# Chunk 0 of the weights in two transfers, its stationary columns rounded on ScalarE, four rounded products first

## What is computed

```
y    = x @ W.T + b + 2 * (x @ A[slot]) @ B[slot]        # slot = itok[sequence], rank 16
base = y @ W_base.T + b_base;  logits = y @ W_router.T
w    = softmax over the two largest logits of 8, placed at their experts
out  = x + base + 2 * sum_e w_e * (y @ A_e.T) @ B_e.T
```

## Time and profile before

| | |
|---|---|
| median of 3 runs | 66.52 us |
| the profiled execution | 66.64 us |
| its span | 64.9 us |
| PE busy | 61.1 us (94%) |
| DVE busy | 36.9 us (57%) |
| ACT busy | 22.9 us (35%) |
| POOL busy | 17.1 us (26%) |

### The profile page before, as it was taken

One profiled execution on the slowest core, in us unless ns is written; L12 is line 12 of the kernel. 1 busy time (PEld: TensorE's weight loads), 2 busy tenths in 40 slices (PEclk: granted clock), 3 DMA queues, 4 the chain that ended last, 5 costly groups with the idle time before them and its releaser, 6 DMA issues.

```text
span 64.9 us, 1174 instructions
## 1 busy us (share of the span) xinstructions
PE 61.1 (94%) x422; PEld 60.2 (93%) x422; DVE 36.9 (57%) x105; ACT 22.9 (35%) x46; POOL 17.1 (26%) x29
## 2 busy tenths in 40 slices
PE   5989999999999999999999999999999999999920
PEld 5969999999999999989999999999999999999910
DVE  0057959999899685126805675012768255956040
ACT  0669078606999898054121100020201131020000
POOL 6700000000799997759360000011000000000000
PEclk9999999999999999999999999999999999999999
DMA  0899998303899305155659997500044000033513
GB/s 0 222 358 353 402 407 267 115 5 96 225 316 374 128 6 130 37 130 126 146 90 399 351 375 282 200 0 0 0 171 154 9 0 0 0 121 121 229 48 127
DMA packets 6025, 10.57 MB, mean 163 GB/s; under 512 B 755, under 2 KB 2547, under 8 KB 6020
## 3 DMA queue, kind: packets, MB, share of 16 engines
q1 hardware_dynamic: 5730, 10.17, 47.1%
q10 hardware_dynamic: 290, 0.33, 1.5%
HBM read 7.37 MB, written 2.10 MB: 146 GB/s over the span
## 4 chain that ended last, share of the span: by engine, by line
PE 89%; DMA 4%; ACT 1%; DVE 1%; DVEq 0%; issue 0%
PE ps L693 26%; PE ps L601 23%; PE ps L705 19%; PE ps L753 8%; PE ps L662 5%; DMA wt<-w_chunks 4%; PE ps L728 2%; PE ps L733 2%; PE ps L739 1%; PE ps L716 1%; ACT wt_hi L352 1%; DVE xn L554 1%; DVEq L71 0%; PE ps L672 0%
## 5 line engine op out<-in xcount | busy, mean ns | idle before, releaser
L693 PE MATMUL ps<-am,x_hi 128*128 128x384 f32 x64 | 16.6, 340 | 0.0
L705 PE MATMUL ps<-bm,x_hi 128*128 128x280 f32 x64 | 13.0, 297 | 0.0
L693 PEld LDWEIGHTS ps<-am,x_hi 128*128 128x128 f32 x64 | 11.4, 188 | 0.0
L693 PE MATMUL ps<-am,x_lo 128*128 128x384 f32 x32 | 10.8, 338 | 0.0
L319 POOL TENSOR_TENSOR x_lo<-xt,x_hi 128x512 fp32r<-128x512 f32 x8 | 10.8, 1361 | 0.0
L705 PEld LDWEIGHTS ps<-bm,x_hi 128*128 128x128 f32 x64 | 10.1, 189 | 0.0
L705 PE MATMUL ps<-bm,x_lo 128*128 128x280 f32 x32 | 9.3, 290 | 0.0
L554 DVE TENSOR_TENSOR xn<-ps,xn 128x280 f32<-128x280 f32 (+1 forms) x16 | 6.1, 418 | 2.7 <-PE ps L753 2.6
L601 PE MATMUL ps<-wt_hi 128*128 128x280 f32 (+1 forms) x32 | 7.0, 316 | 0.2 <-ACT wt_hi L352 0.2
L601 PE MATMUL ps<-wt_lo,wt_hi 128*128 128x280 f32 (+1 forms) x32 | 7.0, 314 | 0.0
L326 POOL CAST am<-as_hl 128x128 fp32r<-128x128 f32 x8 | 2.9, 373 | 14.1 <-PE ps L693 14.1
(11 more groups left out here) (74 smaller groups left out, 99.4 us busy)
## 6 DMA issues: line engine op xcount, KB each, us to landing
xt<-x_t SPq DMA_DIRECT2D x4, 512.0 KB, 6.5
xn<-x_n SPq DMA_DIRECT2D x4, 512.0 KB, 5.5
out_n<-xn SPq DMA_DIRECT2D x7, 256.0 KB, 2.1
wt<-w_chunks SPq DMA_DIRECT2D x2, 582.0 KB, 6.2
g_st<-g_hl SPq DMA_DIRECT2D x12, 81.0 KB, 2.1
ab<-adapters SPq DMA_DIRECT2D x8, 64.0 KB, 2.7
wt<-w_chunks SPq DMA_DIRECT2D x1, 326.0 KB, 4.2
wt<-w_chunks SPq DMA_DIRECT2D x2, 128.0 KB, 3.0
```

Of the source, the lines that this page charges most:

```text
L693: last = mm(a_bank(b)[:, 0:R + WA], v[:, p, i, tok], am[:, i, level, at:at + R + WA], start=(i == 0 and n == 0), stop=False, skip_group_ch ...
L705: mm(b_bank(b)[:, 0:QB], v[:, p, i, tok], bm[:, i, level, :], start=(i == 0 and n == 0), stop=False, skip_group_check=True)
```

## The change

Chunk 0 comes in two transfers, one from SP (all 512 stationary columns) and one from ScalarE (all 648 moving columns and the bias). ScalarE rounds the stationary columns in two halves, blocks 2 and 3 first. VectorE no longer rounds any of them; it takes the remainders of the stationary columns ahead of those of the 368 moving columns. TensorE runs hi by hi for all four blocks, waiting for each half, and then hi by lo for all four.

```diff
-W0_PIECES = [slice(D // 2, D), slice(0, D // 2), slice(D, D + QB), slice(D + QB, CB)]
+W0_PIECES = [slice(0, D), slice(D, CB)]
 # SyncE
-            for n in (0, 1):
-                sp.dma_start(wt[:, 0, W0_PIECES[n]], w[:, 0, W0_PIECES[n]]).then_inc(w0_in[n], 16)
+            sp.dma_start(wt[:, 0, W0_PIECES[0]], w[:, 0, W0_PIECES[0]]).then_inc(w0_in[0], 16)
 # ScalarE
-            for n in (2, 3):
-                act.dma_start(wt[:, 0, W0_PIECES[n]], w[:, 0, W0_PIECES[n]]).then_inc(w0_in[n], 16)
+            act.dma_start(wt[:, 0, W0_PIECES[1]], w[:, 0, W0_PIECES[1]]).then_inc(w0_in[1], 16)
             act.dma_start(idx_sb[:], idx).then_inc(idx_in, 16)
             act.wait_ge(w0_in[0], 16)
-            for i in (2, 3):
-                c = slice(i * P, (i + 1) * P)
+            for c in (slice(D // 2, D), slice(0, D // 2)):
                 hi(wt_hi[:, 0, c], wt[:, 0, c]).then_inc(w0_hi_done, 1)
-            act.wait_ge(w0_in[3], 16)
+            act.wait_ge(w0_in[1], 16)
             hi(wt_hi[:, 0, D + QB:CH], wt[:, 0, D + QB:CH]).then_inc(wc_hi_done, 1)
-            act.wait_ge(w0_in[2], 16)
 # VectorE
-            dve.wait_ge(w0_in[2], 16)
+            dve.wait_ge(w0_in[1], 16)
             nc.vector.tensor_copy(wt_hi[:, 0, b0], wt[:, 0, b0]).then_inc(b0_hi_done, 1)
             dve.wait_ge(b0_hi_done, 1)
             lo(wt_lo[:, 0, b0], wt[:, 0, b0], wt_hi[:, 0, b0]).then_inc(wc_lo_done, 1)
-            dve.wait_ge(w0_in[1], 16)
-            nc.vector.tensor_copy(wt_hi[:, 0, 0:D // 2], wt[:, 0, 0:D // 2]).then_inc(w0_first_done, 1)
+            dve.wait_ge(w0_hi_done, 2)
+            lo(wt_lo[:, 0, 0:D], wt[:, 0, 0:D], wt_hi[:, 0, 0:D]).then_inc(w_lo_done, 1)
             dve.wait_ge(wc_hi_done, 1)
             lo(wt_lo[:, 0, D + QB:CH], wt[:, 0, D + QB:CH], wt_hi[:, 0, D + QB:CH]).then_inc(wc_lo_done, 1)
-            dve.wait_ge(w0_first_done, 1)
-            dve.wait_ge(w0_hi_done, 2)
-            lo(wt_lo[:, 0, 0:D], wt[:, 0, 0:D], wt_hi[:, 0, 0:D]).then_inc(w_lo_done, 1)
 # TensorE
-            for pair in ((2, 3), (0, 1)):
-                if pair[0] == 0:
-                    pe.wait_ge(w0_first_done, 1)
+            for n, pair in enumerate(((2, 3), (0, 1))):
+                pe.wait_ge(w0_hi_done, n + 1)
                 for i in pair:
-                    if i >= 2:
-                        pe.wait_ge(w0_hi_done, i - 1)
                     m_part(0, i, 0, wt_hi, wt_hi, first=True)
-                pe.wait_ge(wc_lo_done, 1)
-                for i in pair:
-                    m_part(0, i, 0, wt_hi, wt_lo)
+            pe.wait_ge(wc_lo_done, 1)
+            for i in range(KB):
+                m_part(0, i, 0, wt_hi, wt_lo)
```

More of the change, by code:

```diff
@@ L176, in build @@
         w0_hi_done = sem("w0_hi_done")
-        w0_first_done = sem("w0_first_done")
         b0_hi_done = sem("b0_hi_done")
```

## The result

In eight executions each, on the same chips, the changed kernel took 68.61 us in the median (67.70 to 69.77) and the kernel before 67.14 (66.47 to 67.40). The changed kernel's times fall in two groups, a quick one of 67.70 to 68.02 (four) and an upper one of 69.21 to 69.77 (four). The ratio, 1.0129 with a 95% interval of 1.0068 to 1.0189, leaves out executions over 1.5% above the fastest of their kernel, and so it is about the quick group alone. The upper group has to be explained as well: the kernel before has nothing above 67.65 in any of its 82 executions here, so it belongs to the change. The direction was forecast, the size was not: 67.05 was predicted, 67.5 was the end of the range.

What follows compares the result with a forecast made beforehand. TensorE was taken to bound the kernel, so a later first product shifts everything: +0.73 us for the merged landing less 0.18 from the order is +0.55 on 66.52, about 67.05 us; range 66.55 to 67.5.

Steps and rivals of the forecast that it cites:

- rival C: TensorE's clock falls to the lower level for chunk 0 after about 0.9 us idle: 67.6 us and up, chance 0.05.
- What bounds the kernel: TensorE, busy 61.1 of 64.9 us: a later first product moves everything behind it, with no idle time to absorb that.
- Merging the transfers: Chunk 0's 326 KB moving transfer lands at 4.50, so VectorE's cast and the first product start later: +0.73 us.
- The stationary columns: SP's 256 KB land at 4.3; ScalarE's two roundings are ready at about 4.71 and 5.05, in time for TensorE.
- rival B: SP's stationary 256 KB land last, at 4.7, so ScalarE's rounding releases the first product at 5.15: 67.35 us, chance 0.07.
- VectorE's and ScalarE's cover: Remainders and later roundings in chunk 0 are ready before TensorE wants them, by 0.24 and 0.2 us for remainders: no cost.
- What the order gives back: Four rounded products ahead of the remainders remove TensorE's wait in chunk 0: 0.18 us gained.
- Queues: SP issues chunks 1 to 3 and the first x tile 0.43 us sooner; they already lie ahead of TensorE, so nothing gained.
- my own late bound: Landing of the 326 KB at 4.8: SP's queue and the earlier next chunk put 0.08 MB more in front, 0.2 us.
- Rival A: The slow first transfer stretch is paid per row, not per byte, so merging is not slower: 66.4 to 66.7 us, chance 0.18.
- The price range: Cost if the clock fell to the lower level for chunk 0's 24 products: +0.5 to +4 us.

Runs made afterwards that it cites:

- 44 constants: Changed kernel with 44 constant matmuls instead of 28 ahead of the first product: 67.61 to 68.17 us in six executions, ratio 1.0138 to the kernel before.
- 14 early constants: Kernel before with 14 constant matmuls instead of 28, leaving the array idle ahead of its first product: 67.97 to 68.83 us, ratio 1.0206.
- SP split: Changed kernel with 44 constants and SP's half of chunk 0 in two 128 KB transfers again: 67.19 to 67.52 us, ratio 1.0051 to the kernel before.
- 30 constants: Kernel before with 30 constant matmuls instead of 28: 66.54 to 67.63 us, ratio 0.9995.
- the added gap: Kernel before, four transfers and 28 constants, first product also waiting for chunk 1's moving columns: 67.67, 70.40, 71.29 and 71.43 us.
- 36 constants: Changed kernel with 36 constant matmuls instead of 28: 67.59 to 67.97 us eight times, and 69.47 and 69.87.
- the wide ones: Kernel before with 7 constant matmuls of 512 columns instead of 28 of 128: 66.65 to 67.53 us, ratio 1.0013.

## Why the prediction was wrong

In short, two steps failed. The sum put the landing at 4.50 and let VectorE's cast release the first product at 4.86; measured were landings of 4.8 to 5.3 and a first product at 5.39 to 5.88 in the six profiles with both halves merged. And rival C, the slow spacing, had a chance of 0.05 and no term in the sum; it took 10 of 16 executions. Part of the distance is the starting point and nothing of the kernel: the three executions of before that I counted from were quick ones, with a median of 66.52, and eight have 67.14.

- **What bounds the kernel: right.** Time follows chunk 1's first product. Against the profile of before it moved by 1.07 (44 constants), 2.69 (changed), 1.79 (14 early constants), 0.59 (SP split), 0.98 (30 constants) and 4.65 us (the added gap), and those executions were 1.07, 2.68, 1.83, 0.59, 0.99 and 4.65 us longer. The one exception is the kernel whose later chunks were held back.
- **Merging the transfers: mechanism right, size wrong.** I gave +0.73 for the first product; it is +1.32 in the profile with 44 constants (5.45 and 4.13) and +1.45 in that of the changed kernel. The failing step is the landing: 4.50 with a late end of 4.8, and 4.83 to 5.16 for the cast's half in six profiles with both merged. I took the same bytes to pass at the rates of before. They don't. The stretches 2.4 to 3.0 and 3.0 to 3.6 (the last column is GB/s), first in the changed kernel:

```profile
2.40:3.00 0.60, 0.60 (x9) 0.60 (x7) 0.00 (x0) 0.60 (x1) 0.60 (x5) 1.00 0.79 230
3.00:3.60 0.60, 0.60 (x8) 0.60 (x7) 0.00 (x0) 0.02 (x1) 0.04 (x1) 1.00 0.96 312
```

and with chunk 1 held back:

```profile
2.40:3.00 0.60, 0.60 (x9) 0.60 (x7) 0.00 (x0) 0.60 (x1) 0.60 (x5) 1.00 0.83 297
3.00:3.60 0.60, 0.60 (x8) 0.60 (x7) 0.00 (x0) 0.04 (x1) 0.03 (x1) 1.00 1.05 415
```

That is 0.33 MB in the changed kernel and 0.43 MB with chunk 1 held back. The kernel before has 0.43 MB as well (327 and 386 GB/s); all seven profiles with four pieces have 0.43 to 0.44, all six with both halves merged and chunk 1 close behind 0.30 to 0.35, and the two with one half merged 0.40 and 0.41. The missing 0.1 MB at 386 GB/s is an estimated 0.26 us, a good part of the 0.33 to 0.66 us by which the landing missed 4.50. Chunk 1's own bytes don't fill the stretch. Packets and MB by queue of the changed kernel, ScalarE's (q10) and SP's (q1), up to 4.0 us and up to 4.4:

```profile
q10 hardware_dynamic: 134, 0.32, 31.2%
q1 hardware_dynamic: 138, 0.28, 20.6%
...
q10 hardware_dynamic: 143, 0.33, 29.5%
q1 hardware_dynamic: 201, 0.42, 27.1%
```

At 4.0 SP's queue had 0.28 MB, hardly more than the 0.26 of its own half, and both together 0.60 MB where they had 0.66 before. ScalarE's last packets come after 4.4. Chunk 1 is issued at 1.20 instead of 1.67, since SP has one transfer less ahead of it; holding it back brings both halves forward by 0.39 us against one profile and puts them ahead of all six. So that chunk 1 close behind two merged transfers costs is shown; how a transfer that has hardly moved a byte slows this stretch is not.
- **The stationary columns: late, as rival B had it**, at 4.78 to 5.32 instead of 4.3. ScalarE's rounding was the last in the changed kernel (5.01 + 0.43, with PE 0.14 behind it), some 0.4 us after VectorE's cast. I had put that release down to rival B and outside the forecast. The two halves land some 0.17 us apart, and which comes first changes: SP's stationary one in three of seven profiles (4.89, 4.78 and 4.50), where VectorE's cast then ends last, and ScalarE's moving one in the others. What a shorter rounding would give where SP's half is second stays open.
- **VectorE's and ScalarE's cover: right.** With the quick spacing no product behind the first waits.
- **What the order gives back: right in place and nearly in size.** 0.25 us (3.90 less 3.65), 0.18 forecast. The first to the ninth product takes 1.10 us, 1.18 forecast. Of the 0.25, 0.09 is not the order's: the first two products stand 0.20 us apart instead of 0.30, since the first one of before was still partly slow and not, as I wrote, starting from idle (with 36 constants and 0.93 us of idle it is 0.20 too). The order itself gives 0.16. On four transfers it gives nothing.
- **Queues: wrong.** "Earlier issue wins nothing there" was right for chunk 1; that it costs chunk 0 was missed in this term, though my own late bound had 0.2 us for it.
- **Rival A, a draw: no.** The slow first stretch did carry more bytes (131 GB/s instead of 92 in 1.6 to 2.4), but 2.4 to 3.0 fell from 327 to 230. The estimate from the Trainium skill, "DMA: Bandwidth & Descriptors", section "Anatomy of one DMA", has the pair land at about 4.1; measured is 4.8 to 5.3. The advice of the same page to coalesce transfers ("Rules for kernel authors") did not pay for these, of 128 to 186 KB.
- **Rival C, the clock: happened in 10 of 16 executions, at a chance of 0.05.** I took the granted clock column at its word, and missed what the timeline of before showed. Its 28 constants of 128 columns take 3.15 us, 0.105 us from one start to the next, and 128 columns at 1.2 GHz are 0.107: the lower level stood there all along, beside a column of 1.00. So I asked whether the level would fall in the gap, where it had not yet risen when the constants ended. No profile here shows chunk 0 go from quick to slow; they differ in when the slow spacing ends. At the quick level constants stand 0.06 us apart. The same shows in durations. A first product of 280 columns lasts 0.37 us in the quick profile with 44 constants, and a constant just ahead of it 0.22:

```profile
5.19 0.22 PE L589 MATMUL ps<-const-bfloat16-1.0 128*128 128x128 bf16 x1
5.45 0.37 PE L593 MATMUL ps<-wt_hi 128*128 128x280 f32 x1
```

It lasts 0.60 in the slow profile with 30 constants:

```profile
4.21 0.60 PE L601 MATMUL ps<-wt_hi 128*128 128x280 f32 x1
```

In the profile of before it lasted 0.46, and the constants 0.31 each to their end. So the spacing turned quick during that very product, and 28 constants had nothing to spare. Of the gap I knew the length to 0.8 us only, because it hangs on the landing. The price range (+0.5 to +4) holds: the upper group lies 1.2 to 2.9 us above the quick one.

Sum of the quick group, from the profile with 44 constants: +1.32 - 0.25 = +1.07 us on the profile of before, and the quickest executions stand 1.1 us apart (67.6 to 67.7 against 66.5 to 66.6). The printed ratio, 0.87 us, is smaller; most likely because the slow spacing raises more than half of the executions of before by up to 1.0 us. Nothing tried beats the kernel before; 30 constants, the wide ones and the new order on four transfers equal it.

## What to carry to other kernels

A flag on a merged transfer rises when all of it is there, here 1.1 to 1.7 us after the first piece's flag, and a transfer issued close behind it made that later still. When the first consumer needs a quarter of the data, split the transfer, and don't take the rates of the old transfers for the new ones. Where constants are run ahead of the first real matmul, they must reach until it starts: a change that delays the first input has to lengthen them too. Look at the spacing of equal matmuls, not at busy share or granted clock, and time enough executions to see whether there are two groups.

## What was not expected of the hardware

- The slow spacing is there with a granted clock of 1.00 in the same stretch: 12 against 22 matmuls in 3 us.
- It is there while the first constants run in every profile, and ends at a different moment in each: during the constants at 3.7 to 5.1 in four of five profiles with 44 of them, by 4.6 in the profile of before, at 6.7 with 30 constants, at 8.9 in the changed kernel and 9.9 in its second profile.
- With 36 constants the last of them is slow (0.31 us) and the first product, 0.93 us of idle later, quick: the level rose while nothing ran.
- Two merged transfers with the next one close behind move 0.30 to 0.35 MB in 2.4 to 3.6 us, four pieces 0.43 to 0.44.
- With one half in one transfer and the other in two, the merged one lands first although it is larger: 326 KB at 4.23 beside 128 KB at 4.41, and 256 KB at 3.98 beside 140 KB at 4.17.
